# bfloat16 copies of the adjacency rows, made by GpSimd in the first layer, and one row load for two heads

## The chip, the cores and the metric

The kernel runs on one core of a Trainium2 chip. The metric is the device time of one execution in microseconds. A core has TensorE (PE), VectorE (DVE), ScalarE (ACT) and GpSimd (POOL), with SyncE (SP) issuing nearly all DMA; they run side by side and wait for each other through semaphores.

## The reference

Four graph layers are applied to `x` (2708 x 256) over one dense 0/1 adjacency matrix `adj` (2708 x 2708, with the diagonal set), each as `x = x + layer(relu(layernorm(x)), adj)`; for the first three:

```
# layer 0: 4 attention heads of 64
scores = leaky_relu(el[:, :, None] + er.T[None], 0.2); where adj == 0: -inf
out    = softmax(scores) @ ht
# layer 1: a GRU over A0 @ h ("edge"), a GRU over the mean of 3 attention heads ("node")
A0 = adj without its diagonal
e_plus = leaky_relu([A0 @ hW, 0] @ a, 0.2)[:, 0]
att    = softmax(where(A0 > 0, e_plus[None, :], -9e15), axis=1); head = (att * A0) @ hW
# layer 2: [h, (adj @ h) / (deg + 1)] @ W.T
```

The softmax of a head in layer 1 needs, for each row i, the largest score among the neighbours of i. As the scores are shifted to be positive, this is the largest product of row i of `A0` with the vector of scores: this is the "row maximum" of which this document treats.

## The kernel before

N = 2816 (22 blocks of 128, `NT` = 22), D = 256. The transposed adjacency stays in SBUF as fp8 (`AT`, 22 x 2816 columns).

**First layer.** Its attention is 12 units (`units0`): 3 groups of target blocks (`GA`: 6, 8 and 8 blocks) by 4 heads. In a unit, each of 22 source blocks j needs a threshold over 768 or 1024 columns (`threshold`, on ScalarE, L869, or on VectorE, L1161, as `threshold_on_act` says), two mask operations of VectorE on fp8 bytes as int32 words (L1193, L1199) and 24 or 32 matmuls (L1674). Six threshold and twelve mask buffers lie between the engines. After a unit ScalarE evicts it (`evict`, L881), at j = 8 of the next one. Of `AT` only the first group is there when this begins, cast by GpSimd (L693). The other 44 chunks of 128x1024 are loaded as float32 by SyncE (`load_chunk`, four buffers `STG`) and cast to fp8 by ScalarE in units 0 to 7 (`cast_chunk`, L859, at `casts_at`). SyncE loads the source scores of unit u+2 (`load_el`) once all thresholds of unit u are through. GpSimd, after its part of the moving operand (L707), next clears the diagonal blocks of `AT` (L715), behind VectorE's `widen` (L1220).

**Edge steps.** Layer 1 first makes h, its halves and their transposes, and the score parts (395 to 461 us). Then 22 edge steps, one for each block t: TensorE does half a support product for a later pair of blocks (L1720, to step 19), the products of all heads (L1732, L1734) and the gates of the GRU (L1759 to L1767). VectorE's loop in a step is written out: a row maximum, the blend of step t-1, more row maxima, the support's low part, the products' low part (L1351), a last row maximum, the new candidate (L1388, L1390). TensorE's products of t+1 wait for the low part of t. SyncE issues, in order, a load of h, the row loads, the save of the products.

**Row maxima.** `row_max(L)` (L1366) multiplies half a row block (128 x 1408 float32, loaded from `adj` into one of three buffers `AROW`, 704 KB) with the head's scores `EB`, broadcast over the partitions, and takes the maximum. The three heads have 44 each, 132 in all, and each loads its rows anew. `rows_before` puts 44 (head 0) in steps 0 to 12, then, with `EB` loaded again, 29 of head 1 in steps 14 to 21; the last 59 stand at every second m of the head loop (`row_at`), those of head 2 with a table of their own, `EB2`, loaded when the edge steps' last block is written. Before the maximum GpSimd clears the diagonal block in the float32 row (`clear_diagonal`, L743). A head's maxima are transposed by TensorE (L1778, L1825), copied, saved and loaded back broadcast (`save_maxima`, `load_maxima`) before the head's exponents.

**Head loop.** 9 units (3 heads by groups of 8, 7, 7 blocks) of 22 sources, m = 0 to 197: exponents on ScalarE or VectorE (L952, L1409), a mask on VectorE (L1419), a power on ScalarE (L961), and 14 or 16 pairs of matmuls (L1812, L1813). At m = 122 and on, checks of the adjacency for layer 4 follow on the same row buffers. Node steps (another GRU, together with layer 2) and layer 2's sum end the kernel.

## Time and profile before

| | |
|---|---|
| median of 3 runs | 1363.55 us (1361.31 to 1370.84) |
| the profiled execution | 1376.85 us, its span 1375.0 us |
| busy: PE, DVE, ACT, POOL | 1187.0, 1000.2, 759.6, 267.6 us |
| mean granted clock of TensorE | 0.935 of full speed |
| DMA | 223.59 MB, 163 GB/s in the mean |
| maxima (L1366) | 132, 1643 ns each, 216.9 us; idle before them 84.1 us |

A row of a group or of the timeline gives the line, the engine, the operation, what it writes and reads, and in brackets or behind the last bar how long its engine sat idle before it and what ended that. Matmuls overlap, so TensorE's busy time is no measure of its peak. Stages, from the span's start: load and first products to 90 us, attention of the first layer to 395, preparation of layer 1 to 461, edge steps to about 728, head loop to 1080, node steps to 1273, layer 2's sum to the end.

### The profile page before, as it was taken

The page shows a single profiled execution, that of the slowest core. Times are in us where ns is not written, and L with a number is a line of the kernel's source. Part 1 is how long each engine was busy: PE and PEld are TensorE (multiplying, and loading weights), DVE is VectorE, ACT ScalarE, POOL GpSimd, SP SyncE. Part 2 cuts the span into 40 slices and gives each one's busy share as a digit, 9 for nine tenths or more (in the row PEclk, how much of TensorE's full clock was granted, in tenths as well). Part 3 has the DMA queues.
Part 4 walks back from the last instruction along what each step waited for, and adds up shares of the span by engine and source line. Part 5 has one row for each costly group of instructions (what it writes and reads, how often), then busy time and mean ns, then how long its engine had stood idle before and what let it go on. Part 6 is the DMA issues. An engine that isn't in the chain of part 4 may idle for free.

```text
span 1375.0 us, 36177 instructions
## 1 busy us (share of the span) xinstructions
PE 1187.0 (86%) x15179; PEld 944.5 (69%) x15179; DVE 1000.2 (73%) x2281; ACT 759.6 (55%) x1142; POOL 267.6 (19%) x340
## 2 busy tenths in 40 slices
PE   4518897999868999999966999997899998988996
PEld 3418897999757766566635888886788654446885
DVE  6587997999985676676776999898995365553641
ACT  3469987998752122222116999896989225553000
POOL 4730000032041022332231110111210042220000
PEclk9759999999975999999977999999999999999998
DMA  9715553211015667768679778676762000020532
GB/s 319 240 70 170 180 148 119 81 34 65 3 49 210 211 205 252 245 215 285 223 251 344 228 247 329 208 248 210 257 223 101 1 28 20 16 92 1 190 107 84
DMA packets 88623, 223.59 MB, mean 163 GB/s; under 512 B 7427, under 2 KB 52345, under 8 KB 88197
## 3 DMA queue, kind: packets, MB, share of 16 engines
q1 hardware_dynamic: 87269, 220.68, 48.5%
q8 instruction: 121, 1.98, 0.6%
q10 hardware_dynamic: 1184, 0.53, 0.1%
q14 instruction: 49, 0.40, 0.1%
HBM read 201.45 MB, written 19.73 MB: 161 GB/s over the span
## 4 chain that ended last, share of the span: by engine, by line
PE 52%; DMA 15%; DVE 14%; ACT 8%; POOL 5%; issue 4%; SPq 1%; DVEq 0%; ACTq 0%; POOLq 0%
PE PS L1674 12%; DMA arena<-in_adj 12%; PE PS L1812 10%; PE PS L1813 10%; PE PS L1866 8%; ACT arena L869 3%; PE PS L1759 3%; DVE scratch L1366 3%; PE PS L1853 2%; PE PS L1766 2%; DVE arena L1139 1%; ACT AT L859 1%; POOL X L734 1%; PE PS L1709 1%; DVE arena L1199 1%
## 5 line engine op out<-in xcount | busy, mean ns | idle before, releaser
L1812 PE MATMUL PS<-arena 128*128 128x257 f16 x1452 | 331.5, 276 | 27.3 <-ACT arena L961 21.6
L1813 PE MATMUL PS<-arena 128*128 128x257 f16 x1452 | 331.3, 278 | 0.0
L1674 PE MATMUL PS<-arena 128*128 128x65 f16 x7744 | 261.8, 196 | 76.1 <-DVE arena L1199 61.4
L1674 PEld LDWEIGHTS PS<-arena 128*128 128x128 fp8e4 x7744 | 258.1, 99 | 79.7 <-issue 59.0
L1366 DVE CUSTOM_DVE_ANT_0 scratch<-arena 128x1408 bf16<-128x1408 f32 x132 | 216.9, 1643 | 84.1 <-DMA arena<-in_adj 48.5
L961 ACT ACTIVATE arena<-arena 128x896 int16<-128x896 uint8 (+1 forms) x198 | 187.4, 972 | 36.3 <-DVE arena L1419 27.5
L869 ACT ACTIVATE arena<-arena 128x1024 fp8e4<-128x1024 f32 (+1 forms) x185 | 189.9, 1089 | 17.7 <-DVE arena L1193 16.9
L1812 PEld LDWEIGHTS PS<-arena 128*128 128x128 bf16 x1452 | 144.2, 99 | 52.8 <-ACT arena L961 18.1
L1813 PEld LDWEIGHTS PS<-arena 128*128 128x128 bf16 x1452 | 141.6, 97 | 23.1
L952 ACT ACTIVATE arena<-arena,E1B 128x896 uint8<-128x896 f32 (+1 forms) x131 | 139.2, 1063 | 13.6 <-DMA arena<-m_rows 13.6
L942 ACT ACTIVATE arena<-arena 128x256 f32<-128x256 f32 x44 | 18.3, 416 | 205.0 <-DVE arena L1390 205.0
L1193 DVE TENSOR_TENSOR arena<-arena,AT 128x256 int32<-128x256 int32 (+1 forms) x264 | 104.8, 397 | 25.3 <-ACT arena L869 18.2
L1759 PE MATMUL PS<-arena 128*128 128x512 f16 x528 | 123.0, 383 | 0.0
L1720 PE MATMUL PS<-AT,arena 128*128 128x256 fp8e4 x968 | 112.1, 276 | 0.0
L1866 PE MATMUL PS<-arena,AT 128*128 128x256 f16 x968 | 106.2, 273 | 0.8 <-DVE X L1520 0.8
L1199 DVE TENSOR_TENSOR arena<-arena,AT 128x256 int32<-128x256 int32 (+1 forms) x264 | 104.1, 395 | 0.0
L1720 PEld LDWEIGHTS PS<-AT,arena 128*128 128x128 f16 x968 | 94.2, 99 | 14.0
L1866 PEld LDWEIGHTS PS<-arena,AT 128*128 128x128 fp8e4 x968 | 94.6, 98 | 12.5 <-DVE X L1520 1.1
L743 POOL TENSOR_TENSOR arena<-arena,NOTI 128x128 f32<-128x128 f32 x66 | 46.0, 697 | 286.2 <-DMA arena<-in_adj 286.1
L1759 PEld LDWEIGHTS PS<-arena 128*128 128x128 f16 x528 | 52.3, 99 | 56.5 <-issue 2.5
L1419 DVE TENSOR_TENSOR arena<-arena,AT 128x224 int32<-128x224 int32 (+1 forms) x198 | 79.8, 428 | 10.8 <-ACT arena L952 10.6
L728 POOL TENSOR_TENSOR arena<-arena 128x256 f32<-128x256 f32 x44 | 32.8, 745 | 256.1 <-ACT arena L942 256.1
(192 smaller groups left out, 1570.7 us busy)
## 6 DMA issues: line engine op xcount, KB each, us to landing
arena<-in_adj SPq DMA_DIRECT2D x176, 704.0 KB, 5.3
arena<-in_adjT SPq DMA_DIRECT2D x44, 512.0 KB, 4.2
hw_saved<-arena SPq DMA_DIRECT2D x22, 387.0 KB, 7.5
arena<-in_adjT SPq DMA_DIRECT2D x22, 384.0 KB, 4.9
arena<-hw_saved SPq DMA_DIRECT2D x9, 774.0 KB, 7.7
arena<-h_saved SPq DMA_DIRECT2D x44, 128.0 KB, 2.1
arena<-e_rows SPq DMA_DIRECT2D x3, 1408.0 KB, 7.1
arena<-el_rows SPq DMA_DIRECT2D x8, 512.0 KB, 5.5
```

The source lines that it names most:

```text
L869: act.activation(THR[:, m % NTHR, 0:nb * P], ELB[:, n % 2, 0:nb * P], ACT.Sigmoid, bias=ERB[:, j, h:h + 1], scale=SHARP, saturate=False).t ...
L952: act.activation(Y[:, m % NRING, 0:nb * P], MB[n % 2][:, 0:nb * P], ACT.Relu, bias=E1B[:, j * H1 + h:j * H1 + h + 1], saturate=False).then ...
L961: act.activation(PWb[:, m % NRING, 0:nb * P], Y[:, m % NRING, 0:nb * P], ACT.Copy, scale=256.0).then_inc(sem("p_ready"), 1)
L1193: dve.tensor_tensor(mask_words(m, 0), THRi[:, m % NTHR, 0:GA[g][1] * P // 4], adj_words(m), ALU.bitwise_and).then_inc(sem("m_plus"), 1)
L1199: dve.tensor_tensor(mask_words(m, 1), mask_words(m, 0), adj_words(m), ALU.bitwise_xor).then_inc(sem("masks_built"), 1)
L1366: dve.tensor_tensor_reduce(junk, AROW[:, L % 3, :], eb[:, c * QUARTER:(c + 1) * QUARTER], 1.0, 0.0, ALU.mult, ALU.max, M2[:, t, c, h:h + 1 ...
L1674: ins = pe.matmul(PS[:, k, q * C0:(q + 1) * C0], MASK[:, (m + j) % NMASK, q, k * P:(k + 1) * P], MOV[:, j, 2 * h + q, a, :], start=(j == 0 ...
L1720: ins = pe.matmul(PS[:, c, 0:D], HHL[:, j, a, c * P:(c + 1) * P], AT[:, j, i0 * P:i1 * P], start=(j == 0 and a == 0), stop=(j == NT - 1 an ...
L1759: pe.matmul(PS[:, bank, :], half(c, a), w[:, c, b, 0:2 * D], start=(first and c == 0 and a + b == 0), stop=False)
L1812: pe.matmul(PS[:, k, 0:D + 1], weights, w[:, 0:D + 1], start=(j == 0), stop=False)
L1813: ins = pe.matmul(PS[:, k, 0:D + 1], weights, w[:, D + 2:2 * D + 3], start=False, stop=(j == NT - 1))
L1866: ins = pe.matmul(o, AT[:, j, t * P:(t + 1) * P], YHL[:, j, a, :], start=(j == 0 and a == 0), stop=(j == NT - 1 and a == 1))
```

## The change

- ScalarE's casts go: GpSimd casts the 44 chunks, SyncE loads them 11 in a unit in units 0 to 3. Of 22 thresholds of each unit from 1 on, 3 are on VectorE (before 9 in units 1 to 7 and 4 in 8 to 11), 19 on ScalarE.
- Behind the chunks, in units 4 to 10, 66 pieces of the adjacency rows (3 for each row block: 1024, 896 and 896 columns) are loaded as float32 (two buffers), the diagonal block is cleared in 22 of them, GpSimd copies each to bfloat16, and SyncE saves it to `AH_D` in DRAM. SyncE issues up to ten pieces in a unit ahead of the load of scores.
- A half-row load is now bfloat16 (352 KB), from `AH_D`, into one of two buffers. In the edge steps it serves the maxima of heads 0 and 1, with two score tables (`EB[:, 0]`, `EB[:, 1]`) loaded before step 0. All 88 stand in steps 0 to 19, 4 or 5 in a step. GpSimd's clearing before each maximum and its wait go.
- The maxima of both heads are negated, transposed (step 20), saved and loaded together. The 44 of head 2 stand at m = 0, 2, 5, 7, ... 107 of the head loop.
- The checks get three float32 buffers (`CROW`) in the same place.

```diff
@@ -59,8 +59,7 @@
...
     AHEAD = 3
-    ROWS_SPLIT = 13
-    ROWS_EDGE = 73
+    ROWS_LAST = 20
     CHECK_FIRST = 122
...
@@ -161,6 +160,11 @@
...
         HTF = AT[:, :, htf_at:htf_at + 4 * H0 * C0].bitcast(F32)
+        ar = Arena()
+        ar.at = stg_at
+        RST = ar.take(2, 1024)
+        RSH = ar.take(2, 1024, dt=BF16, size=2)
+        assert ar.at <= stg_end
         THRi = THR.bitcast(mybir.dt.int32)
...
@@ -170,9 +174,10 @@
...
         rows_at = a1.at
-        EB = a1.take(N)
-        AROW = a1.take(3, QUARTER)
+        EB = a1.take(2, N)
+        AROW = a1.take(2, QUARTER, dt=BF16, size=2)
         rows_end = a1.at
+        CROW = arena[:, rows_at + N:rows_end].rearrange("p (a b) -> p a b", a=3)
         NSH = a1.take(2, DC, 2, 2 * P, dt=F16, size=2)
...
@@ -302,7 +308,7 @@
...
                 return True
-            return j % 5 not in (1, 3) if n < 2 * H0 else j % 5 != 3
+            return j % 7 != 3
         act_thr, dve_thr = [0], [0]
...
@@ -347,36 +353,38 @@
...
-        casts_at = {}
...
+        PAIRED = 2 * 2 * NT
+        MAXIMA = 2 * NT * H1
+
         def rows_before(t):
...
+            return min(PAIRED, -(-PAIRED * t // ROWS_LAST))
+
+        def loads_before(t):
+
+            return max(2, -(-rows_before(t) // 2))
...
+        row_pieces = [(t, g) for t in range(NT) for g in range(len(G0))]
+
+        row_at = {5 * i // 2: 2 * NT + i for i in range(2 * NT)}
...
+        def maxima_after(L):
+
+            return 2 * (L + 1) if L < 2 * NT else PAIRED + L + 1 - 2 * NT
@@ -477,10 +485,33 @@
...
                 load_chunk(n)
+            def save_row(i):
+                t, g = row_pieces[i]
+                b0, nb = G0[g]
+                sp.wait_ge(sem("row_cast"), i + 1)
+                sp.dma_start(AH_D[t, :, b0 * P:(b0 + nb) * P], RSH[:, i % 2, 0:nb * P]
+                             ).then_inc(sem(f"ws_out{2 + i % 2}"), 16)
+
+            def stage_row(i):
+                t, g = row_pieces[i]
+                b0, nb = G0[g]
+                if i == 0:
+                    sp.wait_ge(sem("stg_used"), len(chunk0) - NT)
+                if i >= 2:
+                    sp.wait_ge(sem("row_cast"), i - 1)
+                sp.dma_start(RST[:, i % 2, 0:nb * P], t_in["adj"][t * P:(t + 1) * P, b0 * P:(b0 + nb) * P]
+                             ).then_inc(sem(f"raw{2 + i % 2}"), 16)
+                if i >= 1:
+                    save_row(i - 1)
+
             for u in range(len(units0)):
                 for j in range(NT):
-                    if (u, j) in casts_at and casts_at[(u, j)] + 4 < len(chunk0):
-                        load_chunk(casts_at[(u, j)] + 4)
+                    n = NT + 11 * u + j // 2 + 4
+                    if u < 4 and j % 2 == 0 and n < len(chunk0):
+                        load_chunk(n)
+                    i = 10 * (u - 4) + j // 2
+                    if u >= 4 and j % 2 == 0 and j < 20 and i < len(row_pieces):
+                        stage_row(i)
                     if j == 20 and u + 2 < len(units0):
...
@@ -502,11 +534,11 @@
...
             def load_row(L):
-                h, t, c = row_of(L)
-                if L >= 3:
-                    sp.wait_ge(sem("rmax"), L - 2)
-                sp.dma_start(AROW[:, L % 3, :], t_in["adj"][t * P:(t + 1) * P, c * QUARTER:(c + 1) * QUARTER]
-                             ).then_inc(sem(f"arow{L % 3}"), 16)
+                t, c = half_of(L)
+                if L >= 2:
+                    sp.wait_ge(sem("rmax"), maxima_after(L - 2))
+                sp.dma_start(AROW[:, L % 2, :], AH_D[t, :, c * QUARTER:(c + 1) * QUARTER]
+                             ).then_inc(sem(f"arow{L % 2}"), 16)
             def load_scores(to, h):
...
@@ -526,7 +558,8 @@
...
             sp.wait_ge(sem("bias_e"), 1)
-            load_scores(EB, 0)
+            load_scores(EB[:, 0, :], 0)
+            load_scores(EB[:, 1, :], 1)
             for i in range(8):
...
@@ -558,13 +591,10 @@
...
                     load_h(t + 2, HR, 0)
-                if t == ROWS_SPLIT:
-                    sp.wait_ge(sem("rmax"), 2 * NT)
-                    load_scores(EB, 1)
-                for L in range(rows_before(t + 1) if t else 3, rows_before(t + 2)):
+                for L in range(loads_before(t + 1) if t else 2, loads_before(t + 2)):
                     load_row(L)
                 if t == NT - 2:
-                    save_maxima(0)
+                    save_maxima(0, 2)
                     load_maxima(0)
...
@@ -709,6 +736,24 @@
...
                                    ALU.mult).then_inc(sem("t_d"), 1)
+            pool.wait_ge(sem("mov"), NT)
+            for n in range(NT, len(chunk0)):
+                g, j = chunk0[n]
+                b0, nb = GA[g]
+                pool.wait_ge(sem(f"stg{n % 4}"), 16 * (n // 4 + 1))
+                pool.tensor_copy(AT[:, j, b0 * P:(b0 + nb) * P], STG[:, n % 4, 0:nb * P], saturate=False
+                                 ).then_inc(sem("stg_used"), 1)
+
+            for i, (t, g) in enumerate(row_pieces):
+                b0, nb = G0[g]
+                pool.wait_ge(sem(f"raw{2 + i % 2}"), 16 * (i // 2 + 2))
+                if i >= 2:
+                    pool.wait_ge(sem(f"ws_out{2 + i % 2}"), 16 * (i // 2 + 1))
+                if b0 <= t < b0 + nb:
+                    blk = RST[:, i % 2, (t - b0) * P:(t - b0 + 1) * P]
+                    link(pool.tensor_tensor(blk, blk, NOTI[:], ALU.mult))
+                pool.tensor_copy(RSH[:, i % 2, 0:nb * P], RST[:, i % 2, 0:nb * P]).then_inc(sem("row_cast"), 1)
+
             for t in range(NT):
...
@@ -1353,30 +1364,35 @@
...
                                              op0=ALU.mult, op1=ALU.subtract).then_inc(sem("hw_lo"), 1)
-            def row_max(L):
-
-                h, t, c = row_of(L)
-                dve.wait_ge(sem(f"arow{L % 3}"), 16 * (L // 3 + 1))
-                if diagonal_half(t) == c:
-                    dve.wait_ge(sem("row_diag"), h * NT + t + 1)
+            def row_max(i):
+
+                if i < PAIRED:
+                    L, h = divmod(i, 2)
+                    eb = EB[:, h, :]
+                else:
+                    L, h = i - 2 * NT, 2
+                    eb = EB2
+                t, c = half_of(L)
+                dve.wait_ge(sem(f"arow{L % 2}"), 16 * (L // 2 + 1))
                 dve.wait_ge(sem(f"eb{h}"), 16)
-                if L > 0:
-                    dve.wait_ge(sem("rmax"), L)
-                eb = EB2 if h == 2 else EB
-                dve.tensor_tensor_reduce(junk, AROW[:, L % 3, :], eb[:, c * QUARTER:(c + 1) * QUARTER], 1.0, 0.0,
-                                         ALU.mult, ALU.max, M2[:, t, c, h:h + 1]).then_inc(sem("rmax"), 1)
...
```

## Rows read from the trace of the kernel before

**Rows 1.** Windows by stage: stretch, busy us per engine (instructions), clock, DMA.

```profile
90.00:162.00 72.00, 57.21 (x1619) 56.10 (x1620) 57.18 (x177) 71.00 (x110) 0.00 (x0) 0.88 0.52 156
162.00:395.00 233.00, 204.58 (x6131) 201.99 (x6127) 218.15 (x571) 196.74 (x302) 28.35 (x23) 0.97 0.25 75
461.00:676.00 215.00, 212.48 (x1501) 141.49 (x1500) 152.29 (x280) 44.42 (x109) 59.15 (x78) 1.00 0.73 241
...
739.00:948.00 209.00, 204.93 (x1806) 175.97 (x1807) 196.62 (x380) 189.69 (x207) 29.32 (x32) 0.99 0.74 245
```

**Rows 2.** The timeline, ScalarE evicting units 3 and 10: start, us, form.

```profile
178.54 1.32 ACT L881 ACTIVATE arena<-PS,arena 128x65 f32<-128x65 f32 x6
...
363.08 1.75 ACT L881 ACTIVATE arena<-PS,arena 128x65 f32<-128x65 f32 x8
```

**Rows 3.** The timeline, ScalarE, starts of edge steps 0, 1, 18, 20.

```profile
462.14 0.60 ACT L940 ACTIVATE arena<-PS 128x512 f32<-128x512 f32 x1 [1.70 <-PE PS L1761]
...
473.85 0.60 ACT L940 ACTIVATE arena<-PS 128x512 f32<-128x512 f32 x1 [1.70 <-PE PS L1761]
...
675.96 0.60 ACT L940 ACTIVATE arena<-PS 128x512 f32<-128x512 f32 x1 [1.70 <-PE PS L1761]
...
706.81 0.60 ACT L940 ACTIVATE arena<-PS 128x512 f32<-128x512 f32 x1 [2.32 <-PE PS L1761]
```

**Rows 4.** The timeline, TensorE, start of the head loop.

```profile
728.36 0.37 PE L1812 MATMUL PS<-arena 128*128 128x257 f16 x1 [9.02 <-ACT arena L961]
...
739.11 0.40 PE L1812 MATMUL PS<-arena 128*128 128x257 f16 x1 [5.54 <-ACT arena L961]
```

**Rows 5.** Groups by form, 90 to 395 us, ScalarE and VectorE.

```profile
L859 ACT ACTIVATE AT<-arena 128x1024 fp8e4<-128x1024 f32 x44 | 46.8, 1062 | 0.0
...
L1161 DVE TENSOR_SCALAR arena<-arena 128x1024 fp8e4<-128x1024 f32 x52 | 39.5, 760 | 0.0
L1161 DVE TENSOR_SCALAR arena<-arena 128x768 fp8e4<-128x768 f32 x27 | 16.5, 610 | 0.0
```

**Rows 6.** Groups by form, whole span, GpSimd.

```profile
L743 POOL TENSOR_TENSOR arena<-arena,NOTI 128x128 f32<-128x128 f32 x66 | 46.0, 697 | 286.2 <-DMA arena<-in_adj 286.1
...
L693 POOL CAST AT<-arena 128x768 fp8e4<-128x768 f32 x22 | 18.0, 842 | 3.6 <-DMA arena<-in_adjT 3.4
```

**Rows 7.** The timeline, GpSimd beside VectorE, in first layer and head loop.

```profile
381.53 9.53 POOL L715 TENSOR_TENSOR AT<-AT,NOTI 128x128 fp8e4<-128x128 fp8e4 x8 [51.39 <-DVE AT L1220]
...
999.48 0.38 DVE L1419 TENSOR_TENSOR arena<-arena,AT 128x224 int32<-128x224 int32 x1
...
1000.62 1.09 POOL L676 CAST arena<-arena 128x768 f16<-128x768 f32 x1
1000.96 1.00 DVE L1419 TENSOR_TENSOR arena<-arena,AT 128x224 int32<-128x224 int32 x1
...
1021.60 0.64 POOL L676 CAST arena<-arena 128x512 f16<-128x512 f32 x1
```

**Rows 8.** The page's DMA issues: KB of one, us to landing.

```profile
arena<-in_adjT SPq DMA_DIRECT2D x44, 512.0 KB, 4.2
...
arena<-e_rows SPq DMA_DIRECT2D x3, 1408.0 KB, 7.1
arena<-el_rows SPq DMA_DIRECT2D x8, 512.0 KB, 5.5
```

**Rows 9.** The timeline, VectorE, first and last operation of one edge step's loop.

```profile
544.99 1.63 DVE L1366 CUSTOM_DVE_ANT_0 scratch<-arena 128x1408 bf16<-128x1408 f32 x1 [4.57 <-DMA arena<-in_adj]
...
554.39 0.42 DVE L1390 SCALAR_TENSOR_TENSOR arena<-arena,PS 128x256 f32<-128x256 f32 x1
```

**Rows 10.** The timeline, SyncE's issues of scores and maxima; ScalarE's first exponents.

```profile
714.00 0.38 SPq L544 DMA_DIRECT2D m_rows<-ET  x1
...
724.18 2.19 ACT L952 ACTIVATE arena<-arena,E1B 128x1024 uint8<-128x1024 f32 x2 [8.06 <-DMA arena<-m_rows]
...
734.13 0.42 SPq L512 DMA_DIRECT2D arena<-e_rows  x1
```

More of the change, by code:

```diff
@@ L389, in first_of @@
             return 1 if m % 3 == 2 else 0
-        first_count = [[0], [0], [0]]
+        first_count = [[0], [0]]
         for m in range(3 * 3 * NT):
-            for e in range(3):
+            for e in range(2):
                 first_count[e].append(first_count[e][-1] + (first_of(m) == e))
-        first_sem = ["y_act", "y_dve", "y_pool"]
+        first_sem = ["y_act", "y_dve"]
         units1 = [(h, g) for h in range(H1) for g in range(len(G0))]
@@ L490, in _ @@
             sp.wait_ge(sem("stg_used"), len(chunk0) - NT)
+            save_row(len(row_pieces) - 1)
             for i in range(4):
-                sp.wait_ge(sem(f"ws_out{i}"), 16 * len(range(i, len(pieces), 4)))
+                sp.wait_ge(sem(f"ws_out{i}"), 16 * (len(range(i, len(pieces), 4)) + (len(row_pieces) // 2 if i >= 2 else 0)))
             load_halves(WIHS, 1, "we")
@@ L519, in _ @@
                     load_halves(GWS, 0, "we")
-            for L in range(3):
+            for L in range(2):
                 load_row(L)
@@ L548, in load_maxima @@
                 b0, nb = G0[g]
-                sp.wait_ge(sem("mn"), 16 * (h + 1))
+                sp.wait_ge(sem("mn"), 16 if h < 2 else 32)
                 if n >= 2:
-                    for e in range(3):
+                    for e in range(2):
                         sp.wait_ge(sem(first_sem[e]), first_count[e][(n - 1) * NT])
@@ L579, in _ @@
                         load_products(0, c)
-            for L in range(ROWS_EDGE, ROWS_EDGE + 3):
+            for L in range(2 * NT, 2 * NT + 2):
                 load_row(L)
@@ L597, in _ @@
                 h, g = units1[n]
-                if m in row_at and row_at[m] + 3 < rows_all:
-                    load_row(row_at[m] + 3)
+                if m in row_at and row_at[m] + 2 < 4 * NT:
+                    load_row(row_at[m] + 2)
                 if m + 6 in check_at:
@@ L734, in apply @@
                 pool.tensor_tensor(X[:, t, :], X[:, t, :], hr[:, t % 4, :], ALU.add).then_inc(sem("gru_x"), 1)
-            def clear_diagonal(L):
-                h, t, half = row_of(L)
-                if half == diagonal_half(t):
-                    pool.wait_ge(sem(f"arow{L % 3}"), 16 * (L // 3 + 1))
-                    b = t % (NT // 2)
-                    blk = AROW[:, L % 3, b * P:(b + 1) * P]
-                    pool.tensor_tensor(blk, blk, NOTI[:], ALU.mult).then_inc(sem("row_diag"), 1)
-            for L in range(rows_before(1)):
-                clear_diagonal(L)
             for t in range(NT + 1):
@@ L749, in _ @@
                     delta(t, 0, HR, GT)
-                    for L in range(rows_before(t + 1), rows_before(t + 2)):
-                        clear_diagonal(L)
                 if t >= 1:
@@ L1381, in gru_new, with maxima_turned @@
+            def maxima_turned(h, heads, bank):
+                dve.wait_ge(sem("eT_mm"), 2 if h < 2 else 3)
+                dve.wait_ge(sem("ep") if h == 0 else sem("mn"), 16)
+                dve.tensor_copy(ET[0:heads * NT, :], PS[0:heads * NT, bank, 0:P]).then_inc(sem("mt"), 1)
             def gru_new(t, base, trz, gt):
@@ L1443, in _ @@
                 if t == NT - 2:
-                    maxima_turned(0, PS[0:NT, 0, 0:P])
+                    maxima_turned(0, 2, 0)
                 gru_new(t, 0, TRZ, GT)
```

102 lines of the change are left out of this document (35 added, 67 removed).

## The prediction

> **What bounds the kernel now.** The windows by stage come first [rows 1]. In the attention of the first layer (90 to 395 us) three engines are nearly full together: of 305 us TensorE is busy 57.2+204.6 = 261.8, ScalarE 71.0+196.7 = 267.7, VectorE 57.2+218.2 = 275.4, while GpSimd does almost nothing. In the edge steps (461 to 676) TensorE is busy 212.5 of 215, so the starts of the steps come next [rows 3]: 11.71 us from step 0 to step 1, and 213.8 for 18 steps, or 11.88 each. VectorE does wait for the row loads in there (4.57 us before one maximum, [rows 9]), but TensorE hardly feels it. Only from step 18 to step 20 do the loads bind: 30.85 us. Then come TensorE's waits at the start of the head loop, 9.02 us and 5.54 us [rows 4]; behind them TensorE is busy 204.9 of 209 [rows 1]. So the change takes away a wait that costs little, and it puts its work where three engines are full.
>
> **First layer, what goes and what comes.** ScalarE gives up 44 casts of 1.06 us (46.8, [rows 5]). It takes 46 thresholds from VectorE: 18 in units 1 to 3, 24 in units 4 to 7, 4 behind them. They have the casts' shapes and price, so ScalarE stays where it is. VectorE loses 18 thresholds of 0.61 us and 28 of 0.76 [rows 5], together 32.3, and falls to 275.4-32.3 = 243.1.
>
> GpSimd gets 44 casts of 1024 columns, 66 copies (22 of 1024 columns, 44 of 896) and 22 clearings of a 128x128 block. A cast of 768 columns takes it 0.84 us [rows 6], one of 512 columns 0.64 [rows 7], so 0.2 for 256 columns: I estimate 1.02 us for 1024 and 0.93 for 896. In the old place this engine was idle, and one would cost the work at nothing. But rows 7 show what it does to VectorE. A masking operation of 224 words takes 0.38 us; begun 0.34 us into a GpSimd cast it takes 1.00 and ends 0.25 after it. The cast had 0.75 us to go and VectorE lost 0.62, all but 0.13. The two exclude each other. Nearly all that VectorE does in this stage is such masking with two operands in SBUF. The reverse is there too: of eight clearings released at 381.53 the last ended after 9.53 us, as VectorE's masks ran without a gap until 387.
>
> So their times add. Of each GpSimd operation I take its duration less 0.13: 66x0.89 + 44x0.80 = 93.9, and 22x0.3 for the clearings, 6.6; in all 100.5. Of a clearing, rows 6 show 0.70 with waits in it; 0.3 is what I leave of it without them. The sum 243.1+100.5 = 343.6 has to go into the 305 us: **38.6 us longer**. It takes for granted that VectorE's idle time is filled without a rest, and counts against VectorE its small operations too, which may run beside GpSimd; I let these two cancel and take 38. The bounds: nothing excluded at all gives a gain, below; every GpSimd instruction excluding VectorE for its whole duration gives 66x1.02+44x0.93+22x0.70 = 123.6, and 243.1+123.6-305 = +62.
>
> The Trainium skill, "SBUF — State Buffer", section "SBUF: two separate sides", has a rule for this: a VectorE operation with two SBUF inputs and a GpSimd operation that reads SBUF take the shared port pair as a lock, and who starts first holds it for the whole instruction. By that rule it would be the upper bound, +62; the cast of rows 7 agrees but for its 0.13 us, while the eight clearings that waited for a whole run of masks do not look like taking turns by who asks first.
>
> Why is it not simply late? GpSimd could lag, but SyncE can't: it waits for the conversions before the next load and the next save, and behind ten such pieces stands the load of the source scores for the unit after the next. When it is late, ScalarE's thresholds stop. **The queue alone** has a price too. Two buffers are in flight, and a load goes out only after the conversion of two pieces before and the issue of a save: 0.4+0.4 us of issues [rows 10], 4.2 to landing [rows 8], 1.1 to convert and clear, over two: 3.05 us a piece. The 60 pieces ahead of unit 11's scores take 183 us, and the scores 5.5 [rows 8]; units 4 to 10 take 184.5 now [rows 2]. So even without any exclusion units 4 to 10 can't get shorter. SyncE's 44 chunk loads come earlier, 11 in a unit, and cost nothing: four buffers cover 4.2 us each, and it waits for the cast as before.
>
> Behind the last unit GpSimd has up to 22 clearings of the fp8 diagonal, of which 14 were done early before. They are waited for only by the products of the edge scores; I put them at nothing, within 5 us.
>
> **Edge steps.** A maximum is 1408 elements in 1.63 us [rows 9]. No row has one with a bfloat16 operand; the scores stay float32, and I take the same. Half the time would be the most it could gain, and in steps that TensorE bounds it would be worth nothing. VectorE's loop takes 9.8 us with four of them, 554.81-544.99 [rows 9]; with 4.4 of them at 1.8 it is 10.5, under 11.71. A half-row load is half the size and serves two maxima, so it has 3.6 us and the blend's 1 us to land in; I count no waits.
> - Steps 0 to 18: 3.0 us of waits go (213.8-18x11.71).
> - Step 0 now wants both score tables. The second needs up to 7.1 us more [rows 8], and step 0 has five maxima instead of four; the margin was some 2 us. I take +5, between 2 and 7.
> - Steps 18 to 20: no maxima in step 20, no support products either: 11.71+6.7+0.4 = 18.8 instead of 30.85, so -12.
>
> Step 20 thus begins at 706.8-3+5-12 = 696.8. The maxima of both heads turn there at about +0.3, and from the save at 714.00 to the exponents at 724.18 were 10.2 us [rows 10], from there to the first product of the head loop 4.2 [rows 4]: it begins at 711.5 instead of 728.4.
>
> **The wait that takes its place.** In the head loop's first turn VectorE has the first maximum of head 2, whose scores are loaded only once the last block of the edge steps is written. This load went out at 734.13, 5.8 us after the loop's start, and no one waited for it, because head 1 was still in work. Behind this maximum stand the masks of j=2 and all later ones. Issue at 717.3, landing 7.1 to 11.3 us on (take 8), maximum, mask and power 3: TensorE goes on at 728.4, where it did at 739.1 [rows 4]. So edge steps and the transition give **-11**; 44 instead of 59 maxima in the head loop give -2, as TensorE has only 4 us of idle there [rows 1]. Bounds: -5 (landing late, second table late) to -20 (no wait for the table).
>
> **Sum.** +38-13 = **+25 us**. Against the profiled execution, 1376.85 us, this is 1401.9; the median of the runs stands 13.3 lower, so it is 1388.6. A change within 1% (13.6 us) is what a measurement of this kernel can't tell from none.
>
> **Rivals.**
> - *Faster.* GpSimd's conversions fit into VectorE's gaps. For it: VectorE would have 305-243 = 62 us without work. Against: 100.5 us want to go in. If conversions of one operand excluded nothing, thresholds moved to the right engine and six casts less in unit 0 (6.4 us) would give about -15 there: 1363.6-15-13 = 1335.5. It decides if the masks beside GpSimd's casts take no longer than alone. Chance 0.15.
> - *No change.* A third of the exclusion is covered, because pieces slip into unit 11 and GpSimd reads ahead in the evictions: +13 in the first layer against -13: 1363.6. Chance 0.22.
> - *Slower still.* The queue and the port together: each conversion waits for a gap in the masks, say 1.5 us as a share of the 6 us at 381.53, the period is 3.8, units 4 to 10 take 60x3.8+5.5 = 233.5, +49, and units 0 to 3 with 44 casts +11: 1363.6+60-13 = 1410.6. Chance 0.13.
> - *It doesn't do what it says*: row loads of half the size still come late for two buffers, and VectorE passes 11.71 us a step. One us in each of 20 steps makes it +20 on my sum. It is inside the range.
>
> **The numbers.** My forecast has 0.50: 1388.6, its own range 1375 to 1402. The range over the cases goes from 1340 to 1412: below it lies most of the first rival, above it the worst of the third. Faster by over 1% 0.15; within 1% 0.23, the second rival and the low end of mine; slower 0.62.
>
> **What would show it.** In the profile after, the eviction of unit 10 stands 30 us or more later than 363 us; masks between 200 and 350 us that last 1 us instead of 0.42; ScalarE's thresholds waiting for the scores' load. Wrong if GpSimd's casts run beside masks of unchanged length. Edge steps are right if they begin every 11.71 us from step 1 to 19, and if the first maximum in the head loop waits for the score table and TensorE for it. If step 1 begins on time, my +5 falls.

## The result and the profile after

The change makes the kernel slower: 1427.35 us (median of 4 runs, 1418.89 to 1436.25) against 1366.41 (4 runs beside them), ratio 1.0441, 95% interval [1.0394, 1.0488]. Forecast were 1388.6 us and a range of 1340 to 1412; the direction was right, the size was not. The profiled execution took 1418.89 us (span 1417.1), 42.0 more than that of before. It was the fastest of its four, and that of before, 1376.85, lay above all four runs timed beside the change, so the medians differ by 61. The working below compares the two profiled executions.

SyncE's first load behind the last unit marks the end of the first layer. Before it stood at 395.36 us; timeline of the changed kernel, SyncE:

```profile
457.43 0.27 SPq L529 DMA_DIRECT2D arena<-in_edge_bih  x1
```

So the first layer takes **62.1 us** more. ScalarE's evictions of units 3 and 10, to be read against [rows 2], divide it:

```profile
191.05 2.53 ACT L894 ACTIVATE arena<-PS,arena 128x65 f32<-128x65 f32 x12
...
420.12 1.75 ACT L894 ACTIVATE arena<-PS,arena 128x65 f32<-128x65 f32 x8
```

Units 0 to 3 cost 12.5 us, units 4 to 10 take 229.1 instead of 184.5 us, so 44.5 more, and 5.0 come behind them. The windows that answer to [rows 1] (columns as there):

```profile
90.00:184.00 94.00, 68.41 (x1926) 66.99 (x1927) 86.31 (x192) 76.20 (x118) 62.41 (x44) 0.89 0.71 240
184.00:457.00 273.00, 204.94 (x5824) 199.80 (x5820) 231.41 (x511) 194.99 (x297) 121.28 (x111) 0.91 0.64 197
524.00:740.00 216.00, 212.41 (x1488) 141.35 (x1487) 197.48 (x330) 46.68 (x108) 52.79 (x52) 0.98 0.40 114
```

In 184 to 457 us no engine is full any more: VectorE 231 of 273, ScalarE 195, TensorE 205. TensorE's granted clock was 0.91 in 90 to 457 us against 0.95 in 90 to 395 before, so it spent more of the time at the lower of its two levels, and its busy time is 273.3 against 261.8 us. I take this as a consequence of its waits: in experiment 5 the clock is 0.96 in 184 to 413 us and the layer is still late. No run changes the clock alone. Who waits for whom, 90 to 460 us (engine and line, for whom: us, times, longest):

```profile
PE PS L1688 <- DVE arena L1210: 101.8, 31, 44.8
...
ACT arena L882 <- DMA arena<-el_rows: 43.2, 5, 13.9
...
ACT arena L882 <- DVE arena L1204: 39.9, 28, 6.0
```

TensorE waits 101.8 us for VectorE's masks (61.4 before). ScalarE's thresholds wait 43.2 us for the source scores, which SyncE issues behind ten pieces; before the change they never waited for them. From the load at 220.10 us to that at 402.80, over five units, lie 50 pieces:

```profile
220.10 0.38 SPq L446 DMA_DIRECT2D arena<-el_rows  x1
...
402.80 0.37 SPq L446 DMA_DIRECT2D arena<-el_rows  x1
```

That is 3.65 us a piece (3.05 forecast). The groups by form, 90 to 460 us, show the masks of 256 words (L1204, L1210) and GpSimd's work:

```profile
L1210 DVE TENSOR_TENSOR arena<-arena,AT 128x256 int32<-128x256 int32 x176 | 88.8, 505 | 0.0
L1204 DVE TENSOR_TENSOR arena<-arena,AT 128x256 int32<-128x256 int32 x176 | 86.4, 491 | 37.6 <-ACT arena L882 37.6
...
L744 POOL CAST AT<-arena 128x1024 fp8e4<-128x1024 f32 x44 | 62.4, 1436 | 31.4 <-DMA arena<-in_adjT 28.6 <-DVE arena L1150 2.4
L755 POOL CAST arena<-arena 128x896 bf16<-128x896 f32 x44 | 50.1, 1140 | 62.3 <-DMA arena<-in_adj 61.4
L755 POOL CAST arena<-arena 128x1024 bf16<-128x1024 f32 x22 | 32.9, 1498 | 36.1 <-DMA arena<-in_adj 35.6
L754 POOL TENSOR_TENSOR arena<-arena,NOTI 128x128 f32<-128x128 f32 x22 | 21.4, 972 | 41.7 <-DMA arena<-in_adj 41.7
```

A mask lasts 0.50 us in the mean; 0.41 is its length when nothing is beside it. Both ways of exclusion stand a few us apart in the timeline (VectorE and GpSimd; the last two rows are the first and the last of 13 masks of 0.41 us without a gap):

```profile
252.81 1.00 POOL L755 CAST arena<-arena 128x896 bf16<-128x896 f32 x1 [1.85 <-DMA arena<-in_adj]
252.94 1.15 DVE L1210 TENSOR_TENSOR arena<-arena,AT 128x256 int32<-128x256 int32 x1
...
256.44 5.33 POOL L754 TENSOR_TENSOR arena<-arena,NOTI 128x128 f32<-128x128 f32 x1 [2.63 <-DMA arena<-in_adj]
257.02 0.41 DVE L1210 TENSOR_TENSOR arena<-arena,AT 128x256 int32<-128x256 int32 x1
...
261.04 0.41 DVE L1210 TENSOR_TENSOR arena<-arena,AT 128x256 int32<-128x256 int32 x1
```

The mask that starts at 252.94, inside the cast, loses 0.74 us. The clearing of one block that starts at 256.44 takes 5.33 us, and it is over only when the run of masks is. The shortest casts had the length that the prediction gave them (1.04 us for 1024 columns, 0.93 for 896), the longest took 6.2 us; a clearing, put at 0.3, took 0.45 us at least.

Behind the first layer these two executions differ by 20.0 us in favour of the change; over several executions it is 11 (see the end of the section on the prediction). Starts of edge steps 0, 1, 2, 18 and 20, to be read against [rows 3], and, in step 0, VectorE's second maximum (the first of head 1, which waits for the second score table) and TensorE's wait:

```profile
522.14 0.60 ACT L951 ACTIVATE arena<-PS 128x512 f32<-128x512 f32 x1 [1.70 <-PE PS L1775]
540.23 0.60 ACT L951 ACTIVATE arena<-PS 128x512 f32<-128x512 f32 x1 [2.43 <-PE PS L1775]
551.94 0.60 ACT L951 ACTIVATE arena<-PS 128x512 f32<-128x512 f32 x1 [1.70 <-PE PS L1775]
739.30 0.60 ACT L951 ACTIVATE arena<-PS 128x512 f32<-128x512 f32 x1 [1.70 <-PE PS L1775]
758.03 0.60 ACT L951 ACTIVATE arena<-PS 128x512 f32<-128x512 f32 x1 [1.81 <-PE PS L1775]
```

```profile
525.65 1.63 DVE L1380 CUSTOM_DVE_ANT_0 scratch<-arena 128x1408 bf16<-128x1408 bf16 x1 [4.49 <-DMA arena<-e_rows]
```

```profile
532.54 0.61 PE L1746 MATMUL PS<-arena 128*128 128x512 f16 x1 [3.59 <-DVE arena L1362]
```

Step 0 takes 18.09 us, the 17 from step 1 to 18 take 11.71 each, 18 to 20 take 18.7. Then the head loop's first product, and the wait that answers to [rows 4], with VectorE's maximum ahead of it:

```profile
768.98 0.27 PE L1826 MATMUL PS<-arena 128*128 128x257 f16 x1 [2.14 <-ACT arena L972]
...
787.85 0.40 PE L1826 MATMUL PS<-arena 128*128 128x257 f16 x1 [13.50 <-ACT arena L972]
```

```profile
784.07 1.62 DVE L1380 CUSTOM_DVE_ANT_0 scratch<-arena 128x1408 bf16<-128x1408 bf16 x1 [11.49 <-DMA arena<-e_rows]
```

Against before, step 0 starts 60.0 us late, the head loop 40.6, its second start 48.7, and the end of the span 42.1.

### The profile page after: what moved, and what is told of

The parts are those of the page before. It is cut to its first block, busy times and chain, and to the rows that moved or that the text cites. A ratio compares the mean times of both kernels' runs of the same rounds, so it can differ in the third digit from the quotient of the medians.

```text
span 1417.1 us, 36225 instructions
## 1 busy us (share of the span) xinstructions
PE 1192.2 (84%) x15178; PEld 950.9 (67%) x15178; DVE 1043.4 (74%) x2232; ACT 764.9 (54%) x1144; POOL 380.3 (27%) x406
## 4 chain that ended last, share of the span: by engine, by line
PE 56%; DMA 14%; DVE 13%; POOL 6%; ACT 6%; issue 4%; SPq 1%; DVEq 0%; ACTq 0%; POOLq 0%
PE PS L1826 10%; PE PS L1827 10%; DMA arena<-in_adj 9%; PE PS L1880 7%; PE PS L1734 7%; PE PS L1773 7%; PE PS L1780 4%; PE PS L1688 2%; POOL arena L755 2%; ACT arena L882 2%; PE PS L1746 2%; PE PS L1867 2%; DMA arena<-e_rows 2%; DVE arena L1204 2%; DVE arena L1150 1%
## 5 line engine op out<-in xcount | busy, mean ns | idle before, releaser
L1688 PE MATMUL PS<-arena 128*128 128x65 f16 x7744 | 273.3, 198 | 127.3 <-DVE arena L1210 101.8
L1688 PEld LDWEIGHTS PS<-arena 128*128 128x128 fp8e4 x7744 | 266.8, 101 | 133.8 <-issue 72.4
L1826 PE MATMUL PS<-arena 128*128 128x257 f16 x1452 | 329.4, 275 | 24.6 <-ACT arena L972 18.7
L882 ACT ACTIVATE arena<-arena 128x1024 fp8e4<-128x1024 f32 (+1 forms) x231 | 229.3, 1079 | 83.7 <-DMA arena<-el_rows 43.2
L1380 DVE CUSTOM_DVE_ANT_0 scratch<-arena 128x1408 bf16<-128x1408 bf16 x132 | 223.0, 1689 | 29.4 <-DMA arena<-e_rows 22.2
L972 ACT ACTIVATE arena<-arena 128x896 int16<-128x896 uint8 (+1 forms) x198 | 187.6, 973 | 38.0 <-DVE arena L1435 28.6
L1826 PEld LDWEIGHTS PS<-arena 128*128 128x128 bf16 x1452 | 143.7, 99 | 48.7 <-ACT arena L972 21.5
L1204 DVE TENSOR_TENSOR arena<-arena,AT 128x256 int32<-128x256 int32 (+1 forms) x264 | 127.9, 484 | 44.8 <-ACT arena L882 44.7
L1827 PEld LDWEIGHTS PS<-arena 128*128 128x128 bf16 x1452 | 141.1, 97 | 22.7
L773 POOL TENSOR_TENSOR arena<-arena 128x256 f32<-128x256 f32 x44 | 47.1, 1071 | 378.1 <-ACT arena L953 378.1
L1210 DVE TENSOR_TENSOR arena<-arena,AT 128x256 int32<-128x256 int32 (+1 forms) x264 | 130.1, 493 | 0.0
L755 POOL CAST arena<-arena 128x896 bf16<-128x896 f32 (+1 forms) x66 | 82.9, 1259 | 98.4 <-DMA arena<-in_adj 97.0
L1880 PEld LDWEIGHTS PS<-arena,AT 128*128 128x128 fp8e4 x968 | 94.6, 98 | 12.5 <-DVE X L1534 1.1
```

The lines of the kernel that those rows point to most:

```text
L882: act.activation(THR[:, m % NTHR, 0:nb * P], ELB[:, n % 2, 0:nb * P], ACT.Sigmoid, bias=ERB[:, j, h:h + 1], scale=SHARP, saturate=False).t ...
L972: act.activation(PWb[:, m % NRING, 0:nb * P], Y[:, m % NRING, 0:nb * P], ACT.Copy, scale=256.0).then_inc(sem("p_ready"), 1)
L1204: dve.tensor_tensor(mask_words(m, 0), THRi[:, m % NTHR, 0:GA[g][1] * P // 4], adj_words(m), ALU.bitwise_and).then_inc(sem("m_plus"), 1)
L1210: dve.tensor_tensor(mask_words(m, 1), mask_words(m, 0), adj_words(m), ALU.bitwise_xor).then_inc(sem("masks_built"), 1)
L1380: dve.tensor_tensor_reduce(junk, AROW[:, L % 2, :], eb[:, c * QUARTER:(c + 1) * QUARTER], 1.0, 0.0, ALU.mult, ALU.max, M2[:, c, h * NT + t ...
L1688: ins = pe.matmul(PS[:, k, q * C0:(q + 1) * C0], MASK[:, (m + j) % NMASK, q, k * P:(k + 1) * P], MOV[:, j, 2 * h + q, a, :], start=(j == 0 ...
```

## Experiments

Each was timed beside the kernel before; "first layer" is the end as marked above, in the profiled execution. One such end is uncertain by some us: experiment 11, which leaves the first layer as the changed kernel has it, ended it at 460.42 instead of 457.43.

**1. GpSimd's work alone.** The kernel before, plus

```diff
...
+            for i in range(139):
+                link(pool.tensor_copy(arena[:, hs_at + 768:hs_at + 960].bitcast(FP8), arena[:, hs_at:hs_at + 768], saturate=False))
```

> The kernel before, with 139 conversions of 128x768 float32 to fp8 added on GpSimd from 90 us on, out of and into a piece of SBUF that nobody uses: the same number of columns as the change's 110 conversions, but with no load, no save and no wait of any other engine for them. Theory 1 (the port: a GpSimd conversion and VectorE's masks exclude each other): 139 x (0.84-0.13) = 99 us go into a stage where VectorE has 30 us free, so 60 to 70 us longer, and masks of 1 us instead of 0.42. Theory 2 (the queue: the scores stand behind the pieces in SyncE's queue and ScalarE waits for them): nobody waits here, so within 5 us of the kernel before.

Measured: 1436.69 us, ratio 1.0498 [1.0414, 1.0582], first layer 462.58 (+67.2). By form, 90 to 462 us, casts and the masks of the units beside them:

```profile
L715 POOL CAST arena<-arena 128x768 fp8e4<-128x768 f32 x139 | 119.7, 861 | 11.1 <-DVE arena L1146 2.4
...
L1200 DVE TENSOR_TENSOR arena<-arena,AT 128x192 int32<-128x192 int32 x88 | 65.7, 746 | 2.9 <-ACT arena L875 2.9
L1206 DVE TENSOR_TENSOR arena<-arena,AT 128x192 int32<-128x192 int32 x88 | 65.4, 743 | 0.0
```

The same masks last 0.35 us without the casts: 176 x 0.395 = 70 us, about the whole loss. The casts keep nearly their own length (0.86 us, 0.84 before) with some 0.06 us between them. The first theory holds: the two engines exclude each other, and with work back to back GpSimd wins. VectorE's thresholds of 768 columns are hit as well, 0.92 us instead of 0.61.

**2. The chunk casts alone.** The kernel before with GpSimd's 44 casts and `return j % 7 != 3`, no pieces.

> The kernel before with one part of the change: the 44 casts of chunks on GpSimd, SyncE's chunk loads 11 in a unit, and the thresholds shared 19 to 3. No copies of rows, the maxima as before. Theory 1 (port): 44 x 0.89 = 39 us come to VectorE's port and 32 go, so +7, all of it in units 0 to 3 (about +10 there, and a few us back later). Theory 2 (queue): the four chunk buffers never held the scores up, so -5 to -15.

Measured: 1366.15 us, ratio 0.9978 [0.9938, 1.0018], first layer 395.46. The time is that of the kernel before, between the two theories. The eviction of unit 3 stands at 192.08 us, 13.5 late as in the changed kernel, and the later units, with 32 us of thresholds less on VectorE, win it back. So casts and thresholds together cost nothing, and the 62 us come with the pieces.

**3. The scores' place in the queue.** The changed kernel with

```diff
-                    if j == 20 and u + 2 < len(units0):
-                        load_el(u + 2)
...
+                if n + 2 < len(units0):
...
+                    act.dma_start(ELB[:, n % 2, 0:nb * P].rearrange("p (k q) -> p k q", q=P),
+                                  EL_D[b0:b0 + nb, h2, :].partition_broadcast(P)).then_inc(sem(f"elb{n % 2}"), 16)
```

at the end of ScalarE's unit n.

> The changed kernel, with the load of the next unit's source scores issued by ScalarE at the end of a unit instead of by SyncE behind ten pieces. Nothing else is changed. Theory 2 (queue): ScalarE was idle 43 us before thresholds whose scores were still loading; this goes, and the kernel is 30 to 40 us faster than the changed one, as far as the last pieces don't hold the end up. Theory 1 (port): VectorE's masks are still as long, ScalarE waits for them instead, and at most 15 us come back.

Measured: 1403.66 us, ratio 1.0231 [1.0153, 1.0309], first layer 439.31: 18.1 us less than the changed kernel, more than the port theory allowed (15) and less than the queue theory wanted (30 to 40). The masks of 256 words still last 0.48 us. So neither is all of it.

**4. The copies' work.** The changed kernel with

```diff
...
-                    link(pool.tensor_tensor(blk, blk, NOTI[:], ALU.mult))
-                pool.tensor_copy(RSH[:, i % 2, 0:nb * P], RST[:, i % 2, 0:nb * P])
+                pool.tensor_copy(RSH[:, i % 2, 0:32], RST[:, i % 2, 0:32])
```

> The changed kernel, but GpSimd copies only 32 columns of each of the 66 pieces and clears no diagonal block; all loads and saves of the pieces and SyncE's order stay (left out: the rest of the bfloat16 copies, so the maxima are not the reference's). Theory (port times and queue add up, and the queue's period of 3.64 us is made long by conversions that wait for VectorE): the period falls to about (0.8 of issues + 5 to landing + 0.1)/2 = 2.9 us, 60 pieces take 177 us, less than the 184 of units 4 to 10, and the first layer ends at 395 to 402 us instead of 457; in all 1350 to 1360 us. Rival (the traffic and SyncE's order alone hold the first layer): it ends above 430 us and the kernel takes 1400 us or more.

Measured: 1396.05 us, ratio 1.0172 [1.0104, 1.024], first layer 434.75. The theory (402 us at most) failed; the rival had the first layer right and the time 4 us too long. 22.7 us go, 39.4 stay. The masks of 256 words are back at their length, but GpSimd's copy of 32 columns, 0.28 us in the median, now and then waits for them, up to 6.1 us, and so takes 0.89 in the mean (by form, 90 to 435 us):

```profile
L1207 DVE TENSOR_TENSOR arena<-arena,AT 128x256 int32<-128x256 int32 x176 | 73.4, 417 | 0.0
...
L752 POOL CAST arena<-arena 128x32 bf16<-128x32 f32 x66 | 58.3, 889 | 183.3 <-DMA arena<-in_adj 183.3
```

**5. Both at once.** Experiment 4 with the queue of experiment 3.

> The changed kernel with both at once: GpSimd copies only 32 columns of each of the 66 pieces and clears nothing (left out: the rest of the copies), and the source scores are loaded from ScalarE's queue, no longer behind ten pieces in SyncE's. What stays of the change in the first layer is the traffic of the pieces, 47.6 MB, and GpSimd's 44 casts. Alone, the tiny copies ended the first layer at 434.75 us and the scores' queue at 439.31, against 457.43 with neither and 395.36 before the change. Theory A (a third cost: the traffic delays the loading of TensorE's instructions, whose stalls put down to 'issue' were 24.5 and 30.5 us there and 7.0 before): the first layer still ends 15 to 25 us late, at 410 to 420 us, with issue stalls of 20 us or more; 1370 to 1385 us. Theory B (port and queue are all): it ends at 395 to 400 us, and the kernel takes 1345 to 1358 us.

Measured: 1382.56 us, ratio 1.0123 [1.0072, 1.0175], first layer 412.94. Theory A: 17.6 us stay when the queue is gone and of the copies only 32 columns each are left (0.98 us in the mean). TensorE's waits for "issue" in 184 to 413 us:

```profile
PE PS L1690 <- issue: 20.0, 17, 3.0
```

**6, 7. Traffic alone.** First the kernel before plus, at the start of units 7 to 11,

```diff
+                            sp.dma_start(TR_D[k], t_in["adj"][t * P:(t + 1) * P, c * QUARTER:(c + 1) * QUARTER]
+                                         ).then_inc(sem("traffic"), 16)
```

> The kernel before the change plus traffic that nothing waits for: 20 copies of 704 KB within DRAM (float32 rows to an unused tensor, 29 MB read and written), issued by SyncE, four to a unit, at the start of units 7 to 11 of the first layer, where the DMA share was 0.01 to 0.17 and all chunk loads are through. No work for any engine but SyncE. Theory A (traffic delays TensorE's instruction loading): TensorE's matmuls of the first layer stop at multiples of 128 for 1 to 4 us, put down to 'issue', 10 us or more in all between 250 and 400 us where there were none, and the first layer ends 8 to 18 us later than 395; 1372 to 1385 us. Theory B (traffic costs only through loads that someone waits for): the first layer ends within 2 us of 395, and the time is that of the kernel before.

Measured: 1370.4 us, ratio 1.0008 [0.9972, 1.0043]. The profiled execution, at 1386.89 us the longest of the ten, has theory A's stalls (10 of them, 23.8 us in 184 to 400 us, first layer 407.77), but the timed runs show theory B: 20 copies in units 7 to 11 of the kernel before cost 6 us at most, by the interval. So the same with 32 copies in units 4 to 11, on top of experiment 2:

> The kernel before with GpSimd's 44 chunk casts and the changed thresholds (which alone cost nothing: first layer 395.46 us, 0.9978 of the time before), plus 32 copies of 704 KB within DRAM (46 MB, as much as the pieces move), issued by SyncE four to a unit at the start of units 4 to 11. Nothing waits for them, no engine works for them, the source scores go out ahead of them. Theory A (traffic delays TensorE's instruction loading): between 184 and 400 us stalls of TensorE put down to 'issue' at multiples of 128 matmuls, 15 us or more in all (0 without the copies), the first layer ends 10 to 20 us later, 1376 to 1386 us, ratio 1.008 or more. Theory B (what stays when port and queue are undone is not the traffic): the first layer ends at 395 to 399 us and the ratio stays within 0.995 to 1.004.

Measured: 1385.02 us, ratio 1.0159 [1.0117, 1.0202], first layer 410.27, 14.8 later than without the copies. Three rows of TensorE's timeline, its waits in 184 to 410 us (none for "issue" in experiment 2), and the page's row of one DMA queue (packets, MB, share):

```profile
316.82 4.20 PE L1691 MATMUL PS<-arena 128*128 128x65 f16 x127 [1.41 <-issue]
...
342.56 4.25 PE L1691 MATMUL PS<-arena 128*128 128x65 f16 x128 [1.61 <-issue]
350.13 5.67 PE L1691 MATMUL PS<-arena 128*128 128x65 f16 x128 [3.32 <-issue]
```

```profile
PE PS L1691 <- issue: 20.1, 13, 3.3
```

```profile
q8 instruction: 121, 1.98, 0.6%
```

TensorE stops for up to 3.3 us, with runs of 128 matmuls or a multiple between the stops and no semaphore outstanding. No engine computes for these copies, and no one waits for them in the layer (the last is issued at 339.7 us and lands at most 18.4 later; SyncE waits for them only behind the layer's end). So the traffic is the cause of this loss. What stops is the loading of instructions: the trace's DMA records have each packet of the queue shown, 16384 bytes, some 1 us long. Those ahead of the three rows end at 315.46, 341.25 and 348.77 us, 1.3 to 1.4 us before TensorE goes on. So it is with all 13 stops, and with all 168 stops for "issue" in the first layers of all fifteen traces, from 184 us on: each ends 1.2 to 1.6 us behind the end of such a packet. The packets themselves don't grow with the traffic (median 0.97 us here, 1.16 in experiment 2), so they start late; what holds their start is not shown. The Trainium skill, "Runtime: NRT & Kernel Launch", section "Instruction fetch mechanics", has instructions refilled in blocks of 256 over the engine's own DMA queue, mostly hidden. 128 matmuls with 128 weight loads are one such block, as the trace has it, but here the refill is not hidden.

**8, 9, 10. Copies without GpSimd's work.** The first layer as before; instead of pieces

```diff
...
+            for t in range(NT):
+                pool.dma_start(AH_D[t], t_in["adj"][t * P:(t + 1) * P, :]).then_inc(sem("row_copy"), 16)
```

a conversion within DRAM by GpSimd's DMA queue, the diagonal zeroed in DRAM by SyncE.

> The first layer of the kernel before (casts on ScalarE, thresholds as there), the edge steps and head loop of the changed kernel. The bfloat16 copies of the rows are made by 22 DMAs of GpSimd's queue, DRAM to DRAM with a cast, the diagonal is zeroed in the copy by two DMAs. GpSimd computes nothing for it. If the edge steps' gain is real and the first layer's loss comes from GpSimd's conversions and their queue, the first layer ends near 395 us as before and the whole is about 18 us faster than the kernel before: 1345 to 1352. If the copies' traffic or the writing of GpSimd's descriptors is in the way, the first layer or the start of the edge steps is late by 10 us or more.

Measured: 1406.29 us, ratio 1.027 [1.0203, 1.0338], first layer 437.75, so the loss stays. All copies start at 90 us, the DMA share is 0.98 up to 162, and the chunks come late:

```profile
ACT AT L883 <- DMA arena<-in_adjT: 50.3, 7, 11.1
```

Paced, with `pool.wait_ge(sem("t_act"), act_thr[(4 + t // 3) * NT])` ahead of each, and then with the maxima of head 2 from m = 14 on (experiment 11's edit):

> As the kernel whose row copies are made by 22 converting DRAM-to-DRAM transfers of GpSimd's queue (casts, thresholds and buffers of the first layer as before the change), but the transfers start only in units 4 to 11, three to a unit, instead of all at once at 90 us. Theory (there the 42 us were chunk loads that came late behind the copies' traffic, while the DMA share was 0.98): the first layer ends at 395 to 400 us, edge steps and head loop keep what the change gives them, 18 to 22 us; 1345 to 1352 us. Rival (47 MB of copies slow TensorE's feeding or the source scores wherever they lie): the first layer ends above 410 us, 1362 us or more. Rival 2: the transfers' descriptors, written by GpSimd, hold up VectorE: masks of 1 us beside the issues.

> The paced converting transfers together with the maxima of head 2 from m = 14 on. Theory: the two gains add up, 7 to 10 us below the paced transfers alone: 1337 to 1344 us, ratio to the kernel before 0.98 to 0.985. Rival: the late maxima are worth nothing, 1345 to 1352 us.

Measured: 1388.18 us, ratio 1.0146 [1.008, 1.0212], and 1374.87, 1.0044 [1.0014, 1.0075]; first layers 421.71 and 423.4. The chunks wait 0.5 us now and the masks are 0.42 and 0.45 us long; the losses of 26 and 28 us go with 27.2 and 32.1 us of stalls for "issue" from 184 us on (7.0 in 184 to 395 us before the change). Both forecasts, 1345 to 1352 and 1337 to 1344, failed: also without GpSimd's work these copies make the layer late, at once or paced.

**11. The wait for the score table.** The changed kernel with

```diff
-        row_at = {5 * i // 2: 2 * NT + i for i in range(2 * NT)}
+        row_at = {14 + 12 * i // 5: 2 * NT + i for i in range(2 * NT)}
```

> The changed kernel, but the 44 maxima of head 2 stand at m = 14, 16, 18, 21, ... 117 of the head loop instead of 0, 2, 5, ... 107, so that none of them stands in front of the loop's first masks. Theory (the wait for head 2's score table took the place of the one removed): TensorE's second wait at the start of the head loop, 13.50 us in the changed kernel, falls to the 5 or 6 us that it was before; 7 to 10 us shorter than the changed kernel, 1418 to 1420 us. Rival (TensorE has slack behind this start, or the loop's end is set by the density of the maxima): the wait goes, but the end of the head loop stays, 0 to 2 us. First layer and edge steps do not change.

Measured: 1413.36 us, ratio 1.0312 [1.0249, 1.0375] (1.0441 for the changed kernel), 14 us shorter by the medians, where 7 to 10 were expected. No wait of TensorE over 2.8 us is left in 770 to 1000 us. The pair of experiments 9 and 10 says the same, 13.3 us. By the profiled executions it is less: from the end of the first layer to the end of the span there are 954.0 us against 962.0 (mean of the changed kernel and experiments 3, 4, 5), and 952.3 against 962.6 in the pair.

**12, 13. No copies.** Half rows loaded from the float32 adjacency with a conversion to bfloat16 on the way, by GpSimd's queue:

```diff
+                pool.dma_start(AROW[:, L % 2, :], t_in["adj"][t * P:(t + 1) * P, c * QUARTER:(c + 1) * QUARTER]
+                               ).then_inc(sem(f"arow{L % 2}"), 16)
```

> No copies at all: first layer as in the kernel before; each half row of the edge steps and of head 2 is loaded by GpSimd's queue straight from the float32 adjacency with a conversion to bfloat16 into the changed kernel's two buffers, its diagonal block cleared there by GpSimd, and serves heads 0 and 1 as in the change; maxima of head 2 from m = 14 on. Theory: the first layer ends at 395 us, and of the change only its gains are left: the edge steps' 19 us and the 14 us of the late maxima, less 5 to 10 for loads that start and land later from GpSimd's queue and for clearings that stand in its order before the blends; 1340 to 1352 us, ratio 0.98. Rival (two buffers and GpSimd's own waits make the steps longer than 11.71 us, say 12.5): 17 us more, no gain over the kernel before.

Measured: 1370.87 us, ratio 1.0005 [0.9975, 1.0035], first layer 395.02: no gain, where 1340 to 1352 were forecast. The head loop starts at 716.37 (728.36 before) and loses it again; VectorE in 735 to 1080 us:

```profile
DVE scratch L1382 <- DMA arena<-in_adj: 33.8, 26, 3.0
```

For head 2 the way of before was taken back, three float32 buffers in the place of `CROW`, loaded by SyncE:

```diff
+                sp.dma_start(CROW[:, i % 3, :], t_in["adj"][t * P:(t + 1) * P, c * QUARTER:(c + 1) * QUARTER]
+                             ).then_inc(sem(f"crow{i % 3}"), 16)
```

> As the kernel without copies whose half rows are loaded by GpSimd's queue with a conversion, but for head 2 only the way of the kernel before: float32 half rows loaded by SyncE into three buffers (they lie where the second score table and the bfloat16 buffers were), cleared by GpSimd, maxima from m = 14 on. Theory (there the head loop lost 17 us, VectorE waiting 33.8 us for loads from GpSimd's queue into two buffers): first layer 395 us, head loop begins at 716 as there, and is as long as before; 1346 to 1354 us, ratio 0.985. Rival (the head loop is held by something else, so that starting it 12 to 20 us earlier only moves the wait): 1363 us or more.

Measured: **1356.79 us** (12 runs, 1351.08 to 1362.34), ratio 0.993 [0.9903, 0.9958], first layer 394.27, head loop from 715.35. It beats the kernel before and the changed one, by less than forecast (1346 to 1354): against the kernel before the spans differ by 20.1 us, the medians by 8.7.

## Why the prediction was wrong

- **What bounds, and the sign.** Right: three full engines, and GpSimd's work is not free beside VectorE's masks. Right too that the edge steps' waits cost little.
- **The sum for the first layer, +38, measured +62.1.** This step failed, in two ways. It priced port and queue as alternatives: the port gave the sum, and of the queue I said only that units 4 to 10 "can't get shorter"; their adding up was a rival with a chance of 0.13. And it put the pieces' DMA traffic at nothing, without a reason. The runs give three parts. Traffic: 17.6 us (experiment 5, where the short copies still run; 14.8 in experiment 7). Queue on top: 434.75-412.94 = 21.8. Copies and clearings on top of the traffic: 439.31-412.94 = 26.4. The sum, 65.8, is 3.7 over the 62.1, about what one such end is uncertain by. The third rival named port and queue together and came near by its first layer: +60, of it 11 for units 0 to 3 (measured 12.5) and 49 for units 4 to 10 (44.5). As it had no traffic in it, that it comes so near is partly luck. Luck too is that the upper bound of the port alone, +62, is the measured figure: 18.1 us of it go with the queue (experiment 3).
- **The port, 100.5 us of GpSimd against 305.** Mis-sized in both directions. The masks grew by 49 us in all (257.9 us against 208.9), not by 100; GpSimd itself waited 167 us for loads (28.6+97.0+41.7). VectorE's other operations grew too, which I had let cancel: its thresholds of 768 columns took 1.22 us instead of 0.61. And the waiting comes back through the queue: a clearing put at 0.3 us took 0.97, a cast of 1024 columns put at 1.02 took 1.44 and 1.50. Where the casts ran back to back (experiment 1) the loss was what such a sum says: 99 us into 30 free, and 67.2 measured. The rule of the Trainium skill, "SBUF — State Buffer", section "SBUF: two separate sides", that who starts first holds the ports for a whole instruction, fits the mask at 252.94 us; it does not fit the clearing at 256.44, which stood through 13 masks.
- **The queue, 3.05 us a piece.** Measured 3.65. Landing took 4.4 to 5.1 us instead of 4.2, and conversion and clearing 1.58 in the mean (groups above) instead of 1.1.
- **GpSimd's clearings at the end: 0.** Right within its 5 us: from the end of the first layer to step 0 are 64.7 us, before 66.8.
- **Edge steps.** Right within 1.4 us: 11.71 a step from step 1 on, +6.4 in step 0 (+5 forecast, and by the second table, as said), 18.7 for steps 18 to 20 (18.8). A bfloat16 operand beside a float32 one makes a maximum no faster: 1.62 us.
- **The wait that takes its place.** Right in kind: VectorE's first maximum of head 2 waits for its table and TensorE behind it. The forecast had TensorE's restart 10.7 us earlier against before; it is 60.0-48.7 = 11.3 earlier against step 0. Its price, 8 to 14 us (experiments 11 and 10), was not taken out as a term.
- **The head loop, -2.** By the two profiles 48.7-42.1 = 6.6 less up to the end of the span, which single executions can't tell from 2.
- **All behind the first layer, -13.** Right, by the executions below: -11.

How much the stages behind the first layer give back can be read from more than two traces. From the end of the first layer to the end of the span the same code as before took 979.6, 967.5, 977.0, 977.3 and 963.1 us (the kernel before, experiments 1, 2, 6 and 7), 972.9 in the mean; the changed code took 959.7, 963.3, 962.1 and 963.1 (the changed kernel, experiments 3, 4 and 5), 962.0 in the mean. So the gain is some 11 us and not 20: the one execution of before was long there. Experiment 13, with 960.6, gains 12.3 by this measure and 8.7 by the medians.

What stays open: with 62.1 and 11 the changed kernel should be 51 us slower, and by the medians it is 61. Its profiled execution is 8.5 us below its median; in which stage its other runs lose them is not on record. Nor is it known why 20 copies as traffic cost nothing that can be measured (experiment 6) and 32 cost 1.6% (experiment 7).

## What to carry to other kernels

Work put on an idle engine can have three prices: what it shares with a busy engine (here GpSimd's casts and VectorE's masks, which exclude each other), what it puts ahead of others in a queue, and its DMA traffic. Cost each by itself and sum; here the three came to 65.8 us and the whole to 62.1. In a kernel with a long unrolled TensorE stream, look in the profile for stops put down to "issue" before filling a DMA-quiet stretch. And here the copies were not needed: the best kernel shares each load between two heads without any.

## What was not expected of the hardware

- TensorE stalls for "issue", up to 3.3 us at multiples of 128 matmuls, 20.1 us in 226, when DMA moves 129 GB/s in the mean; none at 29 GB/s (experiments 7 and 2), 7.0 in 211 us at 66 GB/s (the kernel before). Each stop ends 1.2 to 1.6 us behind the end of a 16 KB packet of instructions.
- GpSimd beside gapless masks: a copy of 128x32 takes 0.89 us in the mean (0.28 in the median, 6.1 the longest), a clearing of 128x128 up to 5.33 us. Beside GpSimd's casts without a gap it is the masks that wait, 0.75 us instead of 0.35.
- A transfer that converts float32 to bfloat16 on its way into SBUF lands in 4.6 us for a half row (DMA rows of experiment 12), against 3.0 for the bfloat16 half row from the copy.
